# Per-tile signals for the spread reciprocals, a tail whose attention runs by tiles of 128 tokens, and a new written-out order

## What is computed

```
# stage 1: attention, 16 heads of 16 values
h = layernorm(x) * ln_w + ln_b ;  q, k, v = h @ w_q, h @ w_kv ;  q, k = rope(q), rope(k)
s = q @ k.T / 4
a = (1 + s + s*s/2) / sum(1 + s + s*s/2)       # Taylor softmax
y = (a @ v) @ w_o
x = x + layernorm(y)
# stage 2: a linear layer on quantized operands
f = quantize_fp6_blocks_of_32(layernorm(x)) @ quantize(weight).T + bias
x = x + layernorm(f)
```

## Time and profile before

| | |
|---|---|
| median of three runs | 693.53 us |
| the profiled execution | 693.26 us, its span 691.5 us |
| TensorE (PE) busy | 92% |
| VectorE (DVE) busy | 85% |
| ScalarE (ACT) busy | 82% |
| GpSimd (POOL) busy | 67% |
| mean granted TensorE clock | 0.970 of full |

### The profile page before, as it was taken

The page is one execution under the profiler, slowest core; times in us unless marked ns, Lnnn a source line. Parts: engine busy times, 40 slices in busy tenths (PEclk is TensorE's granted clock), DMA queues, the critical chain, the costliest instruction groups (busy, mean ns, idle before and its releaser), DMA issues. The chain is left out here.

```text
span 691.5 us, 20172 instructions
## 1 busy us (share of the span) xinstructions
PE 635.6 (92%) x6376; PEld 466.3 (67%) x6376; DVE 586.8 (85%) x1424; ACT 563.9 (82%) x1547; POOL 466.1 (67%) x842
## 2 busy tenths in 40 slices
PE   6899989898997989899898989989898998989988
PEld 6666667576675757667575767757576676757678
DVE  5998978798997989799798978979788898977796
ACT  3578979698896979879698988969798797969974
POOL 3674457677785777768676877858677687664464
PEclk9999999999999999999999999999999999999999
DMA  7101120223213132221323232122322212221111
GB/s 230 33 2 46 24 71 17 74 64 79 63 36 82 58 86 71 71 71 32 83 61 86 70 78 64 38 82 57 92 63 70 72 33 56 58 53 55 47 40 47
DMA packets 52359, 43.49 MB, mean 63 GB/s; under 512 B 7200, under 2 KB 48544, under 8 KB 52256
## 3 DMA queue, kind: packets, MB, share of 16 engines
q1 hardware_dynamic: 51440, 41.42, 21.9%
q10 hardware_dynamic: 816, 0.79, 0.3%
HBM read 18.65 MB, written 8.39 MB: 39 GB/s over the span
## 5 line engine op out<-in xcount | busy, mean ns | idle before, releaser
L996 ACT ACTIVATE feat<-ps_f 128x512 f32<-128x512 f32 x256 | 154.4, 606 | 7.4 <-PE ps_f L684 6.7
L537 DVE TENSOR_TENSOR kf<-kf 128x672 f32<-128x672 f32 (+1 forms) x128 | 147.0, 1150 | 0.2
L684 PE MATMUL ps_f<-qT,selr 128*128 128x512 f32 x320 | 139.9, 442 | 0.0
L1588 POOL TENSOR_TENSOR ve_y<-var_y,epst 128x1 f32<-128x1 f32 x64 | 16.2, 253 | 137.8 <-ACT squares_y L1110 137.8
L855 PEld LDWEIGHTS ps_mt<-kf,vp 128*32 128x32 f32 x2048 | 66.1, 110 | 45.1 <-issue 40.0
L855 PE MATMUL ps_mt<-kf,vp 128*32 128x153 f32 x2048 | 79.0, 294 | 4.0 <-POOL kf L1573 2.8
L734 PE MATMUL ps_o<-feat,main 120*32 120x512 f32 x512 | 76.9, 675 | 0.0
L684 PEld LDWEIGHTS ps_f<-qT,selr 128*128 128x128 f32 x320 | 60.9, 191 | 19.8 <-issue 15.9
L640 PE MATMUL ps_w<-wo_h,attT_l 128*128 128x256 f32 x128 | 36.4, 305 | 40.6 <-DVE fb L1463 38.2
L1561 POOL TENSOR_TENSOR qsp<-kf,qsp 128x256 fp32r<-128x256 f32 x64 | 65.6, 1025 | 9.2 <-ACT qsp L1099 6.0
L737 PE MATMUL ps_o<-feat,rm 128*32 128x512 f32 x512 | 71.7, 630 | 0.0
(11 more groups left out here) (185 smaller groups left out, 1979.8 us busy)
## 6 DMA issues: line engine op xcount, KB each, us to landing
xc<-L_attn_x SPq DMA_DIRECT2D x16, 512.0 KB, 4.4
result<-fin SPq DMA_DIRECT2D x64, 128.0 KB, 1.9
xa<-L_attn_x SPq DMA_DIRECT2D x15, 512.0 KB, 4.5
heads_out<-osb SPq DMA_DIRECT2D x224, 32.0 KB, 1.9
shares<-sums SPq DMA_DIRECT2D x112, 64.0 KB
sums<-osb SPq DMA_DIRECT2D x224, 2.0 KB
wkqv<-L_attn_w_kv ACTq DMA_DIRECT2D x2, 256.0 KB, 4.7
xa<-L_attn_x SPq DMA_DIRECT2D x1, 384.0 KB, 5.9
```

Source lines behind the costliest of these rows:

```text
L537: return eng.tensor_tensor(dims(row, F_MAIN, [[FW, heads], [HD, NR - 1], [1, HD]]), dims(row, F_LIN, [[FW, heads], [0, NR - 1], [1, HD]]), ...
L684: pe.matmul(ps_f[i % 2][:, :], selr[:, i], qT[:, par, quad], start=True, stop=True).then_inc(sel_done, 1)
L996: act.activation(feat[:, p2, i], ps_f[i % 2][:, :], ACT.Square).then_inc(squared, 1)
```

## The change

1. `shares_in` becomes four semaphores, one for each tile of a sequence. Each of the eight spreading DMAs adds to its tile's. `normalise_attention` waits for the two DMAs of its own tile; `move_quad` of a sequence's first quad waits for all four.
2. In the last two sequences `select`, `attend` and `copy_quad` work on the 128 tokens of one tile and all four quads, in place of one quad and all 512 tokens. `select` waits for its own tile's queries alone, `turn_quads` for its own tile's copy. `attend` has 32 matmuls of 128 columns in place of 8 of 512, `copy_quad` four ACTIVATEs of 128x128 in place of one of 128x512.
3. LAG, FIRST and FINAL are new, and so are the orders within a step on all engines. TensorE's and ScalarE's lists keep nearly the same order in a circle (`turn_sums` after `turn_q`; `high_q` after `square_3`; `square_k` ahead of `centre`; `high_ffn_input` ahead of `high_h`). SP's `spread_shares` goes ahead of `move_quad`.

```diff
-aT_low_late, inverted, sums_in, shares_in = sem("aT_low_late"), sem("inverted"), sem("sums_in"), sem("shares_in")
+aT_low_late, inverted, sums_in, shares_in = sem("aT_low_late"), sem("inverted"), sem("sums_in"), [sem("shares_in%d" % i) for i in range(NT)]
...
             def step(n):                                   # SP
+                once(n, "invert_sums", spread_shares)
                 each(n, "move_quad", move_quad)
-                once(n, "invert_sums", spread_shares)
                 each(n, "add_ffn", store)
...
                 if quad == 0:
                     wait(sp, norm_ready, NT * (s - 1))
-                    wait(sp, shares_in, 16 * CH * NT * s)
+                    for tile in range(NT):
+                        wait(sp, shares_in[tile], 16 * CH * s)
...
                                      dims(sums[first:first + HC, 0:1], 0, [[0, HD], [1, P]])).then_inc(shares_in[tile], 16)
...
-                    pe.wait_ge(qT_copied, NT * (t.seq + 1))
+                    pe.wait_ge(qT_copied, t.n if t.n > BODY else NT * (t.seq + 1))
...
+                queries = qT[:, par, :, quad * P:(quad + 1) * P] if t.n > BODY else qT[:, par, quad]
...
+                if t.n > BODY:                             # attend
+                    for qd in range(NQ):
+                        part = slice(qd * P, (qd + 1) * P)
+                        for h in range(HQ):
+                            pe.matmul(ps_o[VW * h:VW * (h + 1), part], main[0:NP, par, qd, VW * h:VW * (h + 1)], feat[0:NP, p2, h, part],
+                                      start=qd == 0, stop=False, skip_group_check=True)
+                    for qd in range(NQ):
+                        part = slice(qd * P, (qd + 1) * P)
+                        for h in range(HQ):
+                            mm = pe.matmul(ps_o[VW * h:VW * (h + 1), part], rm[:, par, qd, VW * h:VW * (h + 1)], feat[:, p2, HQ, part],
+                                           start=False, stop=True, skip_group_check=True)
...
-                pe.wait_ge(o_copied, NT * (t.seq + 1))
+                pe.wait_ge(o_copied, t.n)                  # turn_quads
...
+                if t.n > BODY:                             # copy_quad
+                    for qd in range(NQ):
+                        ins = act.activation(osb[:, par, qd, quad * P:(quad + 1) * P], ps_o[:, qd * P:(qd + 1) * P], ACT.Identity,
+                                             bias=cb[:, par, qd:qd + 1])
+                    ins.then_inc(o_copied, 1)
+                    return
...
-                    dve.wait_ge(shares_in, 16 * CH * NT * (t.seq + 1))
+                    dve.wait_ge(shares_in[t.tile], 16 * CH * (t.seq + 1))
```

More of the change, by code:

```diff
@@ L86 @@
[L86 to L92, removed]
+    "warm_up": -20, "fill_a": 0, "sum_features": 3, "select_2": 7, "project_v": 1, "drain_b": 16, "select_3": 7,
@@ L93 @@
+    "low_v": -19, "low_wo": 9, "add_ffn": 17, "inverse_scales": 14, "low_ffn_input": 15, "to_grid": 14,
+    "add_x": 0, "rstd_x": 0, "scale_ln": -20, "tables": -19, "add_f": 17, "rstd_f": 17, "half_turn": 2,
+    "products_2": 2, "low_q": 2, "add_y": 13, "add_s": 14, "rstd_y": 13, "low_attention": 12, "low_h": 0,
+    "rstd_s": 14,
+    "move_quad": 8,
 }
 FIRST = {
-    "turn_z": (-20, -20, -19, -18, -16, -15, -14, -12, -11, -10, -9, -8),
-    "select_0": (-13, -13, -12, -11, -10, -9, -5, 0, 0, 0, 0, 0),
@@ L145 @@
-    "low_h": (0, -21, -20, -19, -16, -13, -11, -10, -9, -6, -5, -4),
-    "move_quad": (-5, -5, -3, -3, 0, 0, 0, 0, 0, 0, 0, 0),
+    "fill_a": (-18, -17, -20, -18, -23, -22, -25, -22, 0, 0, 0, 0),
+    "sum_features": (-19, -18, -18, -15, -11, -9, -6, -4, -3, -2, 0, 0),
+    "select_2": (-12, -9, -6, -4, -3, -2, 0, 0, 0, 0, 0, 0),
+    "project_v": (-20, -19, -19, -18, -17, -15, -10, -8, -6, -4, -3, -2),
+    "select_3": (-11, -9, -6, -4, -3, -2, 0, 0, 0, 0, 0, 0), "select_4": (-10, -8, -6, -3, -3, -2, 0, 0, 0, 0, 0, 0),
@@ L622, in spread_shares @@
                         sp.dma_start(shares[:, c, tile * P:(tile + 1) * P],
-                                     dims(sums[first:first + HC, 0:1], 0, [[0, HD], [1, P]])).then_inc(shares_in, 16)
+                                     dims(sums[first:first + HC, 0:1], 0, [[0, HD], [1, P]])).then_inc(shares_in[tile], 16)
             load_stream(1)
@@ L882, in step @@
                 setup(n, "warm_up", warm_up)
+                early(n, "fill_a", fill)
+                each(n, "sum_features", sum_features)
+                each(n, "select_2", select, 2)
+                each(n, "project_v", project_v)
+                late(n, "drain_b", drain)
+                each(n, "select_3", select, 3)
+                each(n, "ffn", ffn)
+                each(n, "select_4", select, 4)
+                each(n, "turn_q", turn_q)
+                once(n, "turn_sums", turn_sums)
+                each(n, "turn_quads", turn_quads)
+                each(n, "project_kq", project_kq)
                 each(n, "turn_z", turn_z)
                 each(n, "select_0", select, 0)
+                setup(n, "turn_ffn_weight", turn_ffn_weight)
                 each(n, "project_out", project_out)
@@ L1472, in step @@
             def step(n):
+                once(n, "constant", constant)
+                each(n, "stats_x", stats_x)
+                setup(n, "wo_mean", wo_mean)
+                setup(n, "bias_mean", bias_mean)
+                setup(n, "low_kq", low_kq)
+                once(n, "invert_sums", invert_sums)
+                each(n, "moments_x", moments_x)
+                setup(n, "frequencies", frequencies)
+                setup(n, "weight_result", weight_result)
+                each(n, "low_attention_late", low_attention_late)
@@ L1501, in step @@
-                setup(n, "wo_mean", wo_mean)
+                each(n, "extend_k", extend_k)
+                setup(n, "weight_choice", weight_choice)
+                setup(n, "weight_distances", weight_distances)
+                each(n, "products_1", products, 1)
+                setup(n, "ffn_weight_mean", ffn_weight_mean)
+                each(n, "from_grid", from_grid)
+                each(n, "normalise_x", normalise_x)
+                setup(n, "weight_cast_high", weight_cast_high)
+                setup(n, "angles", angles)
```

380 lines of the change are left out of this document (176 added, 204 removed).

## The result

| | before | changed |
|---|---|---|
| median | 692.56 us (690.83 to 693.56, 4 runs) | 650.06 us (648.38 to 650.66, 4 runs) |
| ratio | | 0.9385, 95% interval 0.9356 to 0.9414 |
| span of the profiled execution | 691.5 us | 648.2 us |

The kernel is 42.5 us faster where 55 were forecast; the time is in the range of 622 to 664, and 1 us outside the forecast's own 624 to 649. The wait did go. What was missed is that DVE's work takes longer in the new order, so that DVE bounds the body at 37.2 us a sequence. The signal alone, in the old order, gives 636.3 us.

What follows compares the result with a forecast made beforehand. DVE's wait for the spread shares, stalling TensorE and lowering its clock, was taken as the bound. 693.3 - 58.9 (signal) + 4 (DVE) + 2 (POOL) + 0 - 2 (tail) - 1 (idle matmuls) = 637.4, rounded to 638; range 622 to 664.

Steps and rivals of the forecast that it cites:

- The bound and the signal: Body: DVE's wait for shares stalls TensorE; a signal per tile removes 38.2 us of wait and 20.7 of clock loss, 58.9.
- The rival that the signal frees nothing: Spreading DMAs: the engines serve all eight together, so the first pair lands no earlier; 693 us, chance 0.04.
- (36.2 - 35.9) x 13 = 4 us come back: Body: DVE becomes the next bound at 36.2 us a sequence against TensorE's 35.9, returning 4 us.
- DVE's products get longer: Body: denser POOL work lengthens DVE's four products a sequence; 26 us at most, half of that 651; chance 0.10.
- a mean of the 896 product above 1.3 us: DVE's larger product, L537: a mean duration above 1.3 us would show that POOL lengthens DVE's products.
- the price of 0: SP's queue: spread ahead of `move_quad` costs nothing; the xa load, now issued before the spread, is taken as 0.
- the pair would land 2 us later: Spread behind the xa load: first pair lands up to 2 us later, part of DVE's wait stays; 652 us, chance 0.13.
- The tail: predicted -2: Last two sequences by tiles: up to 9.3 us won, 7.6 paid on ACT's copies; a gain of 2 taken.
- The idle matmuls: End of the span: 14 instead of 26, taking 3.2 us, so the last store ends it; 1 us won.
- POOL, FIRST: `low_h` behind `low_attention` on POOL costs 2 us over 52 steps; new first steps taken as 0, 4 either side.
- the sum's 637.4: Whole kernel: 693.3 with all terms for signal, DVE, POOL, first steps, tail and idle matmuls; rounded to 638 us.

Runs made afterwards that it cites:

- e1: Kernel before with only the spread's semaphore split into four, one per tile; old order and tail: 636.28 us, ratio 0.9206.
- e2: Changed kernel with one count for all eight spreading DMAs again, new order and tail kept: 693.14 us, ratio 1.0013.
- e5: Changed kernel with POOL's instructions in the old order in 32 steps of the body: 665.22 us, ratio 0.9597.
- e6: Changed kernel with DVE's instructions in the old order in 32 steps of the body, POOL's new: 665.65 us, ratio 0.9601.
- e9: Old order on the four engines, signal per tile and tail by tiles, but SP's list new throughout: 650.07 us, ratio 0.9400.
- e10: Changed kernel with SP's queue in the old order, spread ahead of the previous store and xa load: 650.46 us, ratio 0.9407.
- e4: Changed kernel with DVE's second product group for three of six heads from the third tile on, computation incomplete: 629.58 us, ratio 0.9107.
- e11: Changed kernel with two of POOL's products replaced by one-input copies, so some feature values are wrong: 629.04 us, ratio 0.9106.
- e3: Kernel before with the signal per tile and the last two sequences' attention by tiles, old order: 637.78 us, ratio 0.9224.
- e12: Kernel before with the signal per tile and HG = 3 for 2, one head's products moved from DVE to POOL: 649.67 us, ratio 0.9401.

## Why the prediction was partly right

**The bound and the signal: right.** Waits, gaps and clock were one event. Predicted -58.9 + 4 = -54.9 us for the signal in an unchanged order; e1 measured 692.0 - 636.3 = 55.7. DVE arrives 6.4 us after the reciprocal, as said, and the clock rose from 0.970 to 0.995 (e1: 1.0). The rival that the signal frees nothing is out: e2 is the kernel before again. The prediction took 1.86 us a sequence to be lost at the lower clock after the gap; the trace of before has it, a granted clock of 0.64 for the 4.71 us behind the gap, so some 0.36 x 4.71 = 1.7 us, and 1.00 from 299.68 on:

```profile
294.97:299.68 4.71, 4.71 (x26) 1.94 (x30) 4.64 (x14) 2.84 (x9) 3.00 (x8) 0.64 0.22 62
```

**The step that failed: "(36.2 - 35.9) x 13 = 4 us come back. Below that I see no end (DVE's busy time is there whatever the order)."** The mechanism, DVE as the next bound, was right; the term was mis-sized. A sequence takes 37.2 us and not 36.2, and over the 11 sequences of the table that is 10.5 us more than e1. DVE's busy time is not there whatever the order. The same instructions cost it 35.45 us a sequence in e1, 36.64 in the changed kernel and 38.8 in e5. Two things make up the changed kernel's 1.1 to 1.2 us, and the body between the 4th and the 48th tile shows them:

- An instruction's duration depends on what POOL does beside it (e5 moved POOL's list alone, and the durations grew by 2.1 us a sequence). Mean durations of DVE in the body, e1 to the changed kernel: z 0.50 to 0.69, y 0.42 to 0.56, xd 0.64 to 0.71; the other way, the 672 product 1.14 to 0.86 and `att` 0.55 to 0.41. The sum grew by 0.4 us a sequence.

```profile
L540 DVE TENSOR_TENSOR kf<-kf 128x896 f32<-128x896 f32 x42 | 52.0, 1238 | 0.0
L540 DVE TENSOR_TENSOR kf<-kf 128x672 f32<-128x672 f32 x42 | 36.2, 861 | 1.4
L1478 DVE SCALAR_TENSOR_TENSOR xd<-y,rs_s,sc 128x256 f32<-128x256 fp8e4 x42 | 29.8, 711 | 0.0
L1340 DVE TENSOR_SCALAR z<-xa,mv,rs_x 128x256 f32<-128x256 f32 x42 | 29.0, 690 | 0.0
```

- The other 0.7 us is overlap lost. Most of DVE's instructions start some 0.08 us before the one ahead ends. In the changed kernel `rope_add`, `extend_k` and `products_1` stand right behind each other, each waiting for the one ahead and reading what it wrote, and there the next starts 0.03 us after the end (273.03 + 0.68 = 273.71, then 273.74, then 273.99 in the timeline above). `moments_x` behind `stats_x` and `scales` behind `block_maxima` are two more such places. That is 17 times a sequence, and 4 times in e1, where others stand between them. The overlaps (the sum of all durations less the busy time) are 5.4 us a sequence in the changed kernel and 6.1 in e1. They go with DVE's own list and not with POOL's: 5.3 in e5's stretch (POOL's list old), 6.0 in e6's (DVE's list old).

**The rival "DVE's products get longer"** gave 651 and had a chance of 0.10, and the time is 650.1. That the number fits is luck. It is right that POOL's work stretches DVE's, but in sum this makes 0.4 of the 1.1 us; POOL isn't denser (28.8 us a sequence, 30.5 in e1), what stands beside what has changed; the sign, a mean of the 896 product above 1.3 us, didn't come (1.24: 1.20), the 672 product got shorter, and operations that the prediction didn't price grew. The trace that it had could have warned: z had a mean of 0.50 us in the earlier trace rows, while its shortest was 0.40 and its median 0.41, so POOL's effect was there as a mixture.

**SP: the price of 0 held, for the wrong reason.** The prediction weighed the load as a transfer and said that the pair would land 2 us later. It lands hardly later after its issue (e9: 3.0 us in the median). It overlooked that the previous store is also ahead now and that both can be issued late: e9 shows 12 us for that. In the changed kernel nothing of it is left (e10), since there both are issued before the reciprocal has even begun.

**The tail: predicted -2, not there.** The four copies took 1.14 us together, where 1.62 was reckoned from the earlier trace rows; they overlap. After the last of them it is 20.6 us to the end of the last `add_ffn` (28.6 before, 19.3 predicted):

```profile
624.08 1.14 ACT L1113 ACTIVATE osb<-ps_o,cb 128x128 f32<-128x128 f32 x4
```
```profile
643.26 3.29 PE L661 MATMUL ps_f<-one 128*128 128x128 f32 x28
643.47 0.42 DVE L1487 TENSOR_TENSOR fb<-ps_qk,b2c 128x256 f32<-128x256 f32 x1 [1.06 <-PE ps_qk L647]
...
645.36 0.49 DVE L1493 SCALAR_TENSOR_TENSOR fin<-fb,rs_f,xs 128x256 f32<-128x256 f32 x1 [1.08 <-POOL rs_f L1616]
```

From the 48th tile on, though, the changed kernel needs 99.1 us, e1 96.4: 2.7 lost where 2 were to be won. It isn't DVE's stretching, for e4 and e11 have 99.1 and 99.0. Most of it comes with the tail by tiles itself: e3, which differs from e1 by that alone, needs 98.2, and so does e9; e12, without it, needs 96.4. These are single executions, and why it costs 1.8 us stays open, as do the other 0.9. The idle matmuls ended at 646.55 as reckoned (3.29 us for 3.2), ahead of the last store.

**POOL, FIRST: right.** TensorE waited next to nothing for hT_l (2.4 us in 2 times in all), against 2 us predicted. The beginning is 139.9 us, e1's 140.1. It moves with the clock of an execution: in e10, with the same lists on the four engines, it was 137.2 us at a granted clock of 1.00, against 0.98 here.

Together, from the sum's 637.4: less 2.1, for the signal alone gave 636.3 where the sum has 693.3 - 58.9 + 4 = 638.4; + 10.5 for DVE in the body; + 5.7 for the last steps (2.7 lost where 2 for the tail and 1 for the idle matmuls were to be won); - 2 for POOL. That makes 649.5; 650.1 was measured.

**What is left open.** Whether it is the second input or the multiplication of POOL's products that stretches DVE's work; how much of the stretch and how much of the overlap could be had back by an order; what the tail by tiles loses. e1, the kernel before with four semaphores, is the best of the kernels that do the whole computation, 14 us under the changed one; e4 and e11 show that TensorE in the new order would allow 629.

## What to carry to other kernels

Where a wait is removed by finer signals, try that edit alone before a new order: here it made the whole gain, and the new order took a quarter of it back. When the next bound is an engine that is over 90% busy, its busy time is not a constant: look at the spread between the shortest and the mean duration of its operations, and at which of them stand right behind one that they wait for. A reordering that costs nothing may do so only because another bound covers it (e9 against e10), so test it also without the cover.

## What the runs showed of the hardware

- The same DVE instructions in the same order kept DVE busy 36.6 or 38.8 us a sequence, by POOL's order alone (changed kernel, e5).
- DVE's `att` (128x256) took 0.82 us beside POOL's two-input product of 128x224 and 0.42 beside a one-input copy of that size (e4, e11).
- A DVE instruction that waits for the one right ahead started 0.03 us after its end; others started some 0.08 us before it (changed kernel, e1).
- Giving POOL 112 elements more of a product and DVE 112 less made DVE busier, 35.45 to 36.68 us a sequence (e12).
- Eight small DMAs queued right behind a 512 KB load: the first pair landed 3.0 us after its issue in the median (2.9 to 3.5), where the last pair in the kernel before took 2.8 (2.4 to 3.3).
- Four ACTIVATEs of 128x128 took 1.14 us together, one of 128x512 0.67 to 0.72.
